# Exponentials of three heads at a time from two sets of three PSUM banks, and the first batch's maxima one place earlier

## The reference

```
q  = qdq(layernorm(x)) @ qdq(wq).T + bq          # qdq: round to 127 steps of each row's maximum
k, v = split(ctx @ wkv.T + bkv)
o  = softmax(q k.T / sqrt(32)) v                 # 16 heads, 512 x 1024 scores each
x  = x + tanh(g_x) * (qdq(o) @ qdq(wp).T + bp)
h  = layernorm(x)
x  = x + tanh(g_f) * ((silu(h @ gate * gs) * (h @ up * us)) @ down * ds)
```

## Time and profile before

| | |
|---|---|
| median of three runs | 911.02 us |
| profiled execution | 908.2 us |
| its span | 906.4 us |
| PE busy | 852.7 us (94%) |
| DVE busy | 673.0 us (74%) |
| ACT busy | 556.6 us (61%), of it 253.3 us exponentials (300) |
| POOL busy | 252.8 us (28%) |
| units of batch 0 | from 75 to 186 us |
| units of batches 1, 2, 3 | from 325.8, 538.1 and 738.0 us, about 74, 75 and 72 us each |

### The profile page before, as it was taken

One profiled execution on the slowest core, in us unless ns is written; L12 is line 12 of the kernel. 1 busy time (PEld: TensorE's weight loads), 2 busy tenths in 40 slices (PEclk: granted clock), 3 DMA queues, 4 the chain that ended last, 5 costly groups with the idle time before them and its releaser, 6 DMA issues.

```text
span 906.4 us, 13628 instructions
## 1 busy us (share of the span) xinstructions
PE 852.7 (94%) x4974; PEld 314.0 (35%) x4982; DVE 673.0 (74%) x1300; ACT 556.6 (61%) x743; POOL 252.8 (28%) x241
## 2 busy tenths in 40 slices
PE   5989999999999999999899999999999989998998
PEld 1422222244333332234433332224433322234444
DVE  6877967989766788878666778986867778788222
ACT  5557988752466569772555659874356679862330
POOL 1335766872257400020017700002002210020230
PEclk9999999999999999999999999999999999999999
DMA  9334244221211332100111143200010023200001
GB/s 329 105 97 125 84 118 116 80 83 49 50 36 47 99 106 62 44 1 1 44 33 48 38 117 101 67 1 1 15 39 1 1 63 102 53 1 24 12 0 47
DMA packets 37251, 55.29 MB, mean 61 GB/s; under 512 B 8960, under 2 KB 15424, under 8 KB 37184
## 3 DMA queue, kind: packets, MB, share of 16 engines
q1 hardware_dynamic: 35264, 48.13, 18.7%
q0 software_dynamic: 1920, 6.29, 2.3%
HBM read 31.21 MB, written 4.19 MB: 39 GB/s over the span
## 4 chain that ended last, share of the span: by engine, by line
PE 69%; DVE 15%; ACT 8%; issue 7%; DMA 1%; ACTq 0%; DVEq 0%
PE ps L1418 34%; PE ps L1606 9%; PE ps L1586 8%; PE ps L1569 8%; ACT r L907 5%; PE ps L1541 4%; DVE acc L1149 4%; PE ps L1600 4%; PE ps L1614 1%; DVE kst L1124 1%; DVE am L1004 1%; PE ps L1402 1%; DVE xs L1334 1%; DVE r L1290 1%; ACT r L930 1%
## 5 line engine op out<-in xcount | busy, mean ns | idle before, releaser
L907 ACT ACTIVATE r<-ps 128x1024 f32<-128x1024 f32 (+1 forms) x300 | 253.3, 902 | 53.6 <-PE ps L1569 51.1
L1124 DVE CUSTOM_DVE_ANT_0 kst<-ps,kst 128x512 f32<-128x512 f32 x192 | 124.5, 685 | 30.3 <-PE ps L1541 28.9
L1586 PE MATMUL ps<-r,vv 128*32 128x512 f32 x1024 | 137.3, 608 | 3.4 <-ACT r L907 3.2
L1569 PE MATMUL ps<-qst,kst 97*128 97x512 f16 x512 | 138.0, 384 | 2.6 <-ACT r L907 1.4
L1149 DVE TENSOR_TENSOR acc<-acc,r 128x1024 f32<-128x1024 f32 x120 | 138.6, 1215 | 0.0
L861 ACT ACTIVATE kst<-ps 128x1024 f32<-128x1024 f32 x96 | 98.1, 1022 | 54.2 <-PE ps L1474 53.9
L1418 PE MATMUL ps<-xs,w_gate 128*128 128x512 f16 x384 | 91.0, 380 | 2.0 <-DVE xs L1334 2.0
L1418 PE MATMUL ps<-xs,w_up 128*128 128x512 f16 x384 | 91.1, 380 | 0.0
L1569 PEld LDWEIGHTS ps<-qst,kst 97*128 97x128 f16 x512 | 40.5, 97 | 139.3 <-ACT r L907 88.1
L962 ACT ACTIVATE qst<-ps,gs_c 128x512 f32<-128x512 f32 x48 | 33.0, 687 | 68.0 <-PE ps L1418 68.0
L1364 DVE SCALAR_TENSOR_TENSOR xq<-ps,us_c,qst 128x512 f32<-128x512 f32 x48 | 36.0, 749 | 50.6 <-PE ps L1418 50.6
(11 more groups left out here) (173 smaller groups left out, 1347.9 us busy)
## 6 DMA issues: line engine op xcount, KB each, us to landing
kst<-k_reg SPq DMA_DIRECT2D x192, 64.0 KB
qst<-q_reg SPq DMA_DIRECT2D x192, 32.0 KB
xs<-in_x SPq DMA_DIRECT2D x4, 1024.0 KB, 5.9
cf<-in_ctxT POOLq DMA_DIRECT2D x16, 256.0 KB, 3.4
xres<-in_x SPq DMA_DIRECT2D x3, 1024.0 KB, 5.2
out<-xres SPq DMA_DIRECT2D x12, 256.0 KB, 2.0
acc<-in_down_w SPq DMA_DIRECT2D x10, 256.0 KB, 2.6
vv<-in_wkvT SPq DMA_DIRECT2D x2, 1024.0 KB, 9.7
```

The lines of the kernel that those rows point to most:

```text
L907: nc.scalar.activation(prob[:, s:s + heads, :], ps[:, first_bank:first_bank + heads, :], ACT.Exp, scale=SCALE).then_inc(exp_done, 1)
L1124: ins = nc.vector.tensor_tensor_reduce(kept(b, n)[:, k, :], bank(PAIR + k), kept(b, n)[:, k, :], 1.0, -3.0e38, ALU.add, ALU.max, mx[:, g % ...
L1569: mm = nc.tensor.matmul(bank(first_bank + k), kst[0:97, g % 2, j + k, t * P:(t + 1) * P], qst[0:97, g % 2, j + k, :], start=True, stop=True)
L1586: mm = nc.tensor.matmul(ps[j * DH:(j + 1) * DH, O_BANK, :], vv[:, t, h * DH:(h + 1) * DH], prob[:, p_slot(b, u, j), :], start=(t == 0), st ...
```

## The change

There are two parts. **In batches 1 to 3** the 128 heads of a batch are taken in 43 steps of three (the last of two), without regard to units. Scores of three heads go to three banks, (5, 6, 7) and (0, 1, 2) in turn (`THREES`), one exponential reads all three banks, and a set may be written again when the exponentials of two steps earlier are done. The denominators' bank moves from 5 to 3. The PE now issues the scores of step n, and then the values of those units whose last head lies in step n - 2 or before; `totals` of a group comes right after the values of the next group's first unit. **In the prologue** each maxima step moves up by one place: the first D stands right after Q3, V2 carries the steps that V3 had, and so on; `LEAD0` is gone. The six banks of the head of the prologue come in another order, so that the first D finds its banks free. VectorE's last two `q_low` stand behind the first two maxima.

```diff
-FREE_RING, HEAD_RING = (0, 1, 2, 3), (0, 1, 2, 3, 4, 5)
-O_BANK, DEN_BANK, PAIR = 4, 5, 6
+FREE_RING, HEAD_RING = (0, 1, 2, 3), (0, 4, 5, 1, 2, 3)
+O_BANK, DEN_BANK, PAIR = 4, (5, 3), 6
-SCORES = ((0, 2), (0, 6, 2))
+SCORES, THREES = (0, 2), (5, 0)
...
-STEPS0 = {"V2": [[], DIFFS[:1]], "V3": [rest(0), rest(1)], ...
-LEAD0 = rest(9)
+STEPS0 = {"Q3": [DIFFS[:1]], "V2": [rest(0), rest(1)], ...
...
+def three(n):
+
+    return range(3 * n, min(3 * n + 3, UNITS * HG))
...
+                for n in range(STEPS_B if b > 0 else 0):
+                    heads = three(n)
+                    freed = sorted({h // HG - P_RING[1] for h in heads})
+                    if freed[-1] >= 0:
+                        act.wait_ge(p_used, b * UNITS + freed[-1] + 1)
+                    for u in freed:
+                        if u >= 0 and added(b, u):
+                            act.wait_ge(p_dve, add_count(b, u, heads[-1] % HG if u == freed[-1] else HG - 1))
+                    s, first_bank = p_slot(b, 0, heads[0]), THREES[n % 2]
+                    act.wait_ge(s_full, exp_count(b, 0, heads[0]))
+                    nc.scalar.activation(prob[:, s:s + len(heads), :], ps[:, first_bank:first_bank + len(heads), :],
+                                         ACT.Exp, scale=SCALE).then_inc(exp_done, 1)
...
+            def scores_of_three(b, n):
+                first_bank = THREES[n % 2]
...
+                if n >= 2:
+                    pe.wait_ge(exp_done, STEPS_0 + (b - 1) * STEPS_B + n - 1)
+                elif first_bank == DIFF + 1:
+                    pe.wait_ge(diff_kept, (b + 1) * len(DIFFS))
                     pe.wait_ge(m_free, FREE_AFTER[b, STREAM[-1]])
                 else:
+                    for k in range(3):
+                        products_done(b, first_bank + k)
+                for k, h in enumerate(three(n)):
+                    mm = score(b, h // HG, h % HG, first_bank + k)
                 mm.then_inc(s_full, 1)
...
+                for n in range(STEPS_B + 2 if b > 0 else 0):
+                    if n < STEPS_B:
+                        scores_of_three(b, n)
+                    while done < UNITS - 1 and (done * HG + HG - 1) // 3 <= n - 2:
+                        values(b, done)
+                        sums(b, done)
+                        if done % MT == 0 and done > 0:
+                            totals(b, done // MT - 1)
+                        done += 1
```

More of the change, by code:

```diff
@@ L142 @@
 AHEAD_EARLY = (2, 2)
-STREAM0 = [s for n in A_SEQ0 for part in STEPS0.get(n, []) for s in part] + LEAD0 + UNIT_LIST0
+STREAM0 = [s for n in A_SEQ0 for part in STEPS0.get(n, []) for s in part] + UNIT_LIST0
 assert [s for s in STREAM0 if s[0] == "D"] == DIFFS
@@ L909, in _ @@
                     if t == 0 and g > 0:
-                        act.wait_ge(o_full, b * G + g)
-                        nc.scalar.copy(oT[:, g - 1, :], bank(O_BANK)).then_inc(o_out, 1)
-                    if b == 0:
-                        projection_weights(u)
+                        turned_out(b, g)
+                    projection_weights(u)
+                for n in range(STEPS_B if b > 0 else 0):
[10 more added lines that the diff above has]
+                                         ACT.Exp, scale=SCALE).then_inc(exp_done, 1)
+                    for h in heads:
+                        g, first = divmod(h - HG + 1, MT * HG)
+                        if first == 0 and g > 0:
+                            turned_out(b, g)
                 act.wait_ge(p_used, (b + 1) * UNITS)
-                nc.scalar.copy(denT, bank(DEN_BANK)).then_inc(den_out, 1)
+                nc.scalar.copy(denT, bank(DEN_BANK[b > 0])).then_inc(den_out, 1)
                 nc.scalar.copy(oT[:, G - 1, :], bank(O_BANK)).then_inc(o_out, 1)
@@ L1245, in _ @@
                     key_difference(0, 1)
-                for part in STEPS0.get(f"V{n}", []):
+                for k, part in enumerate(STEPS0.get(f"V{n}", [])):
                     maxima(0, part)
+                    if n == len(EARLY_V):
+                        q_low(0, CT - 2 + k, a_free)
                 w_magnitudes()
-            maxima(0, LEAD0)
             for b in range(B):
@@ new lines, in score, with scores @@
+                return nc.tensor.matmul(bank(out), kst[0:97, g % 2, j, t * P:(t + 1) * P], qst[0:97, g % 2, j, :],
+                                        start=True, stop=True)
+            def scores(u, j):
+                first_bank = score_bank(u, j)
+                if u % MT == 0 and j == 0:
+                    stacked(0, u // MT)
+                if u == 0 and j < 2:
+                    pe.wait_ge(v_out, v_out_count(f"V{MT - 1}"))
+                elif single(0, u) or u > SINGLES:
+                    pe.wait_ge(exp_done, exp_count(0, u, j) - 2)
+                elif first_bank == DIFF0:
+                    pe.wait_ge(diff_kept, len(DIFFS))
+                else:
+                    pe.wait_ge(exp_done, exp_count(0, u - 1, HG - 1))
+                for k in range(1 if single(0, u) else 2):
+                    mm = score(0, u, j + k, first_bank + k)
+                mm.then_inc(s_full, 1)
@@ L1565, in scores @@
                 else:
-                    for k in range(2):
-                        released(b - 1, [n for n in d_seq(b - 1) if d_bank(b - 1, n) == first_bank + k][-1])
-                for k in range(1 if single(b, u) else 2):
-                    mm = nc.tensor.matmul(bank(first_bank + k), kst[0:97, g % 2, j + k, t * P:(t + 1) * P],
-                                          qst[0:97, g % 2, j + k, :], start=True, stop=True)
+                    for k in range(3):
+                        products_done(b, first_bank + k)
@@ L1576, in values @@
                 if u == 0 and b == 0:
-                    pe.wait_ge(m_free, FREE_AFTER[0, next(s for s in LEAD0[::-1] if s[0] == "R")])
+                    pe.wait_ge(m_free, FREE_AFTER[0, ("R",) + DIFFS[_first - 1][1:]])
                 if u == 0:
@@ L1666, in _ @@
                 q_product(bank(A_BANK[f"Q{n}"]), n, a_full)
+            for part in STEPS0[f"Q{CT - 1}"]:
+                for s in part:
+                    maxima(0, s)
             for n in range(len(EARLY_V), MT):
                 first_v(n)
-            for s in LEAD0:
-                maxima(0, s)
             pe.wait_ge(rows_set, 1 + G)
@@ L1675, in _ @@
                 last = b == B - 1
-                for u in range(UNITS):
-                    g, t = divmod(u, MT)
-                    scores(b, u, 0)
-                    scores(b, u, 1 if single(b, u) else 2)
+                for u in range(UNITS if b == 0 else 0):
+                    scores(u, 0)
+                    scores(u, 1 if single(b, u) else 2)
                     if u >= 1:
@@ L1682, in _ @@
                     if single(b, u):
-                        scores(b, u, 2)
-                        scores(b, u, 3)
-                    for s in UNIT_MIDS0.get(u, []) if b == 0 else []:
+                        scores(u, 2)
+                        scores(u, 3)
+                    for s in UNIT_MIDS0.get(u, []):
                         maxima(b, s)
```

79 lines of the change are left out of this document (39 added, 40 removed).

## The result

The changed kernel takes 918.38 us in the median (917.52 to 923.00, 7 runs) against 911.02 (908.71 to 913.33, 7 runs): a ratio of 1.0091, 95% interval 1.0073 to 1.0109. It is slower, by 7.4 us in the median.

The account below looks back on a forecast made before the run. The PE was taken to bound plain stretches, VectorE the ends of groups in batches 1 and 2. Prologue, batch and stacked-key terms summed to +9.7 us: 908.2 becomes 917.9, plus 2.8 to the median, 920.5; range 914 to 925.

Parts of the forecast that it names:

- The exponential of three: ScalarE, batches 1 to 3: a three-bank exponential takes about 1.45 us, the next starting after 1.345.
- Rival 2: The long exponential costs a pair and a single, 1.61 us, so ScalarE exceeds the PE: +5, 925.5 us; chance 0.10.
- The start of a batch: First scores of batches 1 to 3: PE idle 1.75 us instead of 0.88, +0.87 each; batch 3 also gets -0.9.
- Behind `totals`: After `totals` in each later batch, scores wait for exponentials that overwrite heads an addition still reads: +2.3 us a batch.
- the batch's end: At a batch's end the waits for the last two exponentials come to about 1 us either way: 0.
- VectorE's return in batches 1 and 2: Earlier first additions remove waits for the last one: 2.1 us of waits instead of 2.6 to 2.9, -0.7 each.
- rival 1: VectorE decides: batches 1 and 2 lose all their waits, the change is faster: -5.0, 906 us; chance 0.09.
- The stacked keys: Group key copies start later and land 1.4 to 2.5 us after issue: +1.0 us in all, bounds 0 and 3.
- The prologue: Second D and an R in V3 come late, first scores at 77.3 instead of 75.01: +1.5 us, bounds -1.4 and +2.4.
- rival 4: The clock falls to 1.2 GHz after the PE idles 2.7 us in the prologue: +2.2, 922.5 us; chance 0.04.
- From the profiled execution to the median: The median lies 2.8 us above the profiled execution, so a forecast 917.9 becomes 920.5.
- The rule on long instructions: ScalarE isn't saturated but causes bubbles elsewhere, so by the skill's rule the long exponential can only add bubbles.

Follow-up runs that it names:

- Alone the half: The kernel before with only the prologue's half of the change, exponentials of batches 1 to 3 still in pairs: 912.19 us, ratio 1.0010.
- `totals` early: The changed kernel with `totals` of batch 3 one unit earlier, behind `sums` of the group's last unit: 918.53 us, ratio 1.0085.
- `totals` first: The changed kernel with `totals` ahead of the values of a group's first unit instead of behind them: 914.76 us, ratio 1.0048.
- sums by pairs: The changed kernel with `totals` giving sums back by pairs of heads, the first addition waiting for the fourth matmul only: 919.44 us, ratio 1.0098.
- additions that don't wait for `totals`: `totals` multiplies rows of V instead of VectorE's sums: in the changed kernel 912.30 us, ratio 1.0016; in the kernel before 909.45 us, 0.9982.
- `totals` later: The kernel before with `totals` behind the scores of a group's second unit instead of ahead of them: 903.45 us, ratio 0.9930.

## Why the prediction was right, step by step

It said slower by 9.7 us. The profiled executions differ by 10.0, the medians by 7.4. The direction and the mechanism were right. That 10.0 and 9.7 lie so near is in part luck: some 0.9 us of the 10.0 is the clock, as the steps on the prologue and the clock show. The reasons in the prediction's order:

**The exponential of three: right.** 1.45 us (1452 ns in the middle, 1444 in the mean), the next after 1.35. Rival 2 falls.

**The start of a batch: right.** In batch 1 the third set comes 1.06 later than it could (330.53, where six scores from 328.17 on are through after 1.30), the fourth 0.69; forecast 1.05 and 0.7. In batch 3 the sum is the same, but 0.31 of it stands ahead of the second set, which waits for VectorE's read of bank 0: the six scores are drawn 1.77 long instead of 1.46. With the block of values and the six scores that now stand ahead of the first `totals` taken off, the 21.58 us from first scores to there are 0.97 more than the old 18.21; forecast 0.87. The 0.83 us of the old start of batch 3 is gone, as forecast.

**Behind `totals`: right in place and size.** The scores wait 0.49 two steps later in group 1, 0.38 in group 2, twice 0.52 in group 3, all behind an exponential held by an addition; with what they are drawn short 2.6 us a batch, forecast 2.3. The last group is nevertheless only 0.68 longer than before in batch 3 (14.87 and the 2.40 that `totals` moved, against 16.59), so about 0.7 comes back at the batch's end, where I had 0. The kernel whose additions don't wait for `totals` shows it as cause; that `totals` ahead of the values takes waits away there agrees. This is the step that makes the change slower: a long exponential fits a ring of 12 heads without a wait only if it touches no head that an addition still reads. The prediction read that off a count of heads.

**VectorE's return in batches 1 and 2: right, a little small.** The waits of `totals` for it fall from 5.1 to 1.1 us; what is left is 0.36 at the last `totals` of each batch. In batch 1 scores at 364.95, 367.81 and 381.49 wait 0.99, 0.19 and 0.36 for ScalarE behind an addition, some 2.1 us with what they are drawn short; the prediction had 2.1, 0.5 of it at each junction:

```profile
364.95 0.82 PE L1581 MATMUL ps<-qst,kst 97*128 97x512 f16 x3 [0.99 <-ACT r L937]
```

The waits that went were a little larger than I had them: the chain's row starts the first `totals` at 344.17, the timeline at 343.99, so from there to the next it was 19.27 and not 19.09. The two batches are 2.4 and 2.0 longer, where 2.5 was forecast. So rival 1's gain was there, and smaller than what the additions cost elsewhere.

**The stacked keys: right in batch 3.** Scores wait for the shift's row until 2.6 us after its issue, a little above my 1.4 to 2.5, and that costs 0.4 at 777. The rest of the forecast 1.0 is not pinned to the keys by a row; at 796.16 scores wait another 0.30 for ScalarE. The three experiments that take other waits out of batch 3 run into the keys twice each, at 0.5 to 1.1.

**The prologue: the term was right, the clock lies over it.** The Relu behind the cut (ends at 51.76, forecast 51.83), R at 58.31 (58.8), the next two such R in steps of 4.39 and 4.38 (62.70, 67.08), the wait for the first exponential from 1.10 to 0.47: as forecast. First scores are at 76.96, not 77.3, 1.95 later than before; less the 0.63 of the shorter wait that is +1.3, forecast +1.5. From there the R in batch 0, first before, then after:

```profile
77.51 0.39 PE L1541 MATMUL ps<-k_reg,q_reg 32*128 32x512 f16 x2
82.51 0.39 PE L1541 MATMUL ps<-k_reg,q_reg 32*128 32x512 f16 x2
100.37 0.39 PE L1541 MATMUL ps<-k_reg,q_reg 32*128 32x512 f16 x2 [0.39 <-DVE crow L1111]
78.84 0.39 PE L1570 MATMUL ps<-k_reg,q_reg 32*128 32x512 f16 x2
82.45 0.39 PE L1570 MATMUL ps<-k_reg,q_reg 32*128 32x512 f16 x2
101.00 0.39 PE L1570 MATMUL ps<-k_reg,q_reg 32*128 32x512 f16 x2 [0.51 <-DVE crow L1140]
```

The kernel before runs at half clock from 78 us on, and by 82.5 its lead is gone. Then the changed kernel falls 0.6 behind again: its chain of waits names VectorE from 83 us on, that of the kernel before only from 90. From the first R to the last one shown it takes 22.86 us and the changed kernel 22.16, so the stretch at 78 costs 0.7. The changed kernel's own stretch, at 235, costs 1.6, and that makes the +0.6 at 101 us a +2.4 at batch 1. Without both stretches it would be about +1.5 there, and the two profiled executions would differ by some 9.1 us. Alone the half measured +1.0 by the medians, which is not clear of noise. At equal mean clock it is more, 911.9 us (five executions at 0.996) against 910.0 (twelve).

**The clock, rival 4: my reason against it was wrong.** I had read that the PE idles 6.3 of 19 us near the end at full clock and concluded that the clock does not fall. It falls in the kernel before, in a place that the prediction did not read, and in the changed one elsewhere; not at the 2.15 us of idle time in the prologue that the rival named. Windows of 2 us (PE busy, PEld, DVE, ACT, POOL, granted clock, DMA share, GB/s), first the kernel before:

```profile
76.00:78.00 2.00, 1.20 (x7) 0.39 (x7) 0.46 (x3) 2.00 (x6) 1.92 (x3) 0.98 1.01 379
78.00:80.00 2.00, 2.00 (x10) 0.31 (x9) 2.00 (x6) 1.76 (x4) 0.52 (x1) 0.50 1.12 287
80.00:82.00 2.00, 2.00 (x14) 0.29 (x10) 1.07 (x3) 1.14 (x3) 0.81 (x1) 0.67 0.70 164
```

and the changed kernel:

```profile
232.00:234.00 2.00, 0.35 (x3) 0.15 (x4) 1.55 (x3) 0.00 (x0) 2.00 (x2) 1.00 0.20 49
234.00:236.00 2.00, 2.00 (x10) 0.86 (x9) 0.00 (x0) 1.35 (x2) 1.71 (x2) 0.78 0.46 107
236.00:238.00 2.00, 2.00 (x6) 0.45 (x4) 0.75 (x1) 0.36 (x1) 0.00 (x0) 0.50 0.47 110
238.00:240.00 2.00, 2.00 (x12) 0.77 (x12) 1.26 (x4) 1.02 (x1) 0.00 (x0) 0.87 0.47 108
```

Each of these two profiled executions has one stretch at 1.2 GHz. Both come behind idle time: 1.10 us ending at 76.70, and 1.76 us ending at 233.65, after which the PE ran for another 1.4 us at full clock. The Trainium skill, TensorE: Matmul & The Clock Gate, Part 1, has the clock fall back when the array idles; the traces agree that far. But the same 1.76 us is there in the kernel before, at 231.14, and 2.15 us at 51.81 in the changed one, both at full clock. In three experiments with the same prologue (`totals` early, `totals` first, sums by pairs) the clock did fall at 52 us. So the same idle time was followed by a stretch in some executions and by none in others. The one at 235 us costs 1.6 us, where the rival had 2.2, and as the kernel before has one too, only some 0.9 of it shows between the two traces.

**From the profiled execution to the median: the step that failed.** I added 2.8 us, since the old median lies that far above its profiled execution (the sum then gives 920.7; the prediction's 920.5 is a slip of 0.2). But those 2.8 us belong to the clock of that one execution, not to every kernel. Over the 63 executions of the kernel before in the three sets, the time goes with the mean granted clock:

| mean granted clock | 0.998 | 0.996 | 0.994 | 0.991 | 0.988 |
|---|---|---|---|---|---|
| executions | 8 | 12 | 32 | 4 | 3 |
| mean us | 908.6 | 910.0 | 911.0 | 913.1 | 914.7 |

(The other four lie between.) The profiled one was at 0.998, the usual one is at 0.994. The changed kernel had five of seven at 0.998, mean 918.3, so its median lies only 0.2 above its profiled execution. At equal mean clock it is 9.7 us slower; the medians hide 2.3 of that. The mean clock is a rough measure, though, since a stretch at 78 us costs 0.7 and one at 235 us 1.6. So 920.5 was 2.1 too high through the offset: the terms alone were some 0.6 too large, if the two stretches are taken out.

**The rule on long instructions.** The Trainium skill, Perfetto Trace Analysis, section Optimizing Scalar/DVE Operations, would break up the instructions of an engine that is not saturated and makes others idle. The traces agree: with no wait for an addition left, batch 1 has 71.1 us with the long exponentials (additions that don't wait for `totals`) and 69.6 with the short ones (`totals` later). The two kernels differ in the place of `totals` as well, so the 1.5 us between them is not the length's alone. The waits behind `totals` make most of the rest of the change's cost, and the kernel with short exponentials and late `totals` has none of them.

## What to carry to other kernels

Count which buffers a longer instruction overwrites and who still reads them: an engine with time to spare becomes the one that is waited for when one of its instructions must wait for a slower reader. Before you change a size, try where the instruction stands that releases the slower reader: two lines that let `totals` stand behind one more unit's scores were worth 6.6 us, the rewritten exponentials cost 7. Compare executions at equal granted clock, and check where each trace ran slowly, before a difference of under 1% is given to an edit.

## What had not been expected of the hardware

- The granted clock falls to 1.2 GHz one to five times in a profiled execution. Where it does differs between kernels whose work is the same but for shifts of a microsecond or two: at 78 us before, 235 us after, and at 52, 80, 203, 235, 331, 546, 577 or 845 us in the experiments. In the chain of waits of the changed kernel twelve product matmuls then take 4.16 us instead of 2.70:

```profile
234.04 4.16 PE ps L1447 x12
```

  Not every stretch costs that much. With the new prologue it is 24.02 to 24.04 us from the first scores of batch 0 to the R near 101 us in four kernels without a stretch there, and 24.63 to 24.96 in six with one between 76 and 83 us, so there it costs 0.6 to 0.9. VectorE, which the chain of waits names behind it, may hide the rest; that is not shown.
- A four-head block of 32-column f32 matmuls (`totals`), eight of 592 ns, is through in 1.04 us, and a signal after its fourth matmul brought the reader in 1.08 us after the block's start instead of 1.11: nothing was gained from releasing the first half early.
